# A bidirectional Mamba layer: group 0 of a step on other engines

## The chip, the cores and the metric

The kernel runs on all 8 cores of one Trainium2 chip, each core with one sequence of the batch of 8 and no exchange between them. The metric is the time of the slowest core in microseconds (us), the median of several runs. Lower is better. A core has TensorE (PE, matmuls), VectorE (DVE), ScalarE (ACT), GpSimd (POOL) and the SyncE queue (SP), from which most DMAs are issued here. Each follows its own queue of instructions in order; semaphores tie the queues together.

## The reference

Layer norm, a forward and a backward Mamba block, a projection of both, and a gate from a feed-forward net with ternary weights:

```
xz = x @ win.T;  u, z = split(xz)
u = silu(causal_conv4(u) + bconv)
dbc = u @ wx.T            # dt (64 columns), B (16), C (16)
delta = softplus(dt @ wdt.T + bdt)
dA  = exp(delta[..., None] * A)
dBu = (delta * u)[..., None] * B[:, :, None, :]
h = dA_t * h + dBu_t ;  y_t = sum_n h[:, n] * C_t[n]      # scan over 2048 positions
y = (y + u * Dp) * silu(z);  return y @ wout.T

s = concat(mamba_f(xn), flip(mamba_b(flip(xn)))) @ wproj.T + bproj
g = silu(relu(xn @ Wq1.T + b1) @ Wq2.T + b2)     # Wq: weights rounded to -1, 0, 1
out = x + s * g
```

Sizes of a core: 2048 positions, 1024 model columns, 2048 inner channels, 16 states to a channel, 4096 feed-forward columns.

## The kernel before

Positions are cut into 4 chunks of 512 (`TC`), inner channels into 16 tiles of 128 partitions (`NET`). A **step** s is one channel tile of one chunk of one direction: 2 x 4 x 16 = 128 steps (`NSTEP`), forward first. The 16 states of a step are four **groups** of four (`g` = 0 to 3, `G` = 4 s + g), and a group is two **halves** (pairs) of two states, 1024 columns. Chunks after the first of a direction start from the states carried over from the chunk before ("carried" steps, 96 of 128).

For one group the work is:

- `exp_dA` (L597): ScalarE writes exp(delta A) for each state to one PSUM bank; banks 0 to 3 are two pairs, used in turn by the halves. Column `first(s)` of a state is left at zero, so that a scan over two states starts anew at the second.
- `dbu_half` (L574): GpSimd multiplies `du` (delta times u, from `du_mul`, L562, on VectorE) by B, which lies broadcast over partitions in `Bsl`, into the slot of the group in `hb` (4 slots of 2048 bf16 columns). `fix_b`, `fix_c`, `fix_add` (L622 to L638) add the carried states at the first column.
- `scan` (L648): VectorE, dA from PSUM, dBu and the result in `hb`.
- `h_carry` (L661) saves the last column (ScalarE; VectorE for group 3), `c_mul` (L677) multiplies the slot by C on VectorE, 2048 columns in place, and `y_acc` (L692) sums the four states into PSUM bank `YB` with identity matmuls.
- After group 3, `gate` (L708) multiplies by silu(z) on VectorE.

Around it runs the rest, placed by hand in the main loop (for `s`, for `g`): the u and z projections of later steps (`u_mm`, `z_mm`: 8 matmuls each), the convolution by diagonals (`conv_mm`), delta two steps ahead (`delta_mm`, `delta_exp`: a clamp and an exponential, `delta_ln`), `dbc_mm` and the broadcasts of B and C once a chunk, and in the background the feed-forward net and the output projection (`pe_units`, one unit of 8 matmuls to a group, its result taken out by ScalarE from `act_evacs`) and the rounding of the weights (`act_stream`, ScalarE, 192 operations). Nothing is scheduled by a program at run time: each engine's queue is the order of the calls. `dbu_half` waits for a given C product (its argument `Gc`), which keeps GpSimd's products behind VectorE's.

The order of the main loop around the change, per group G: two exponentials; evacuations, `u_silu`, `z_silu` and others by group; two exponentials; background unit; in group 0 `du_mul(s + 1)`, `h_carry`, `c_mul(G - 1)`, `y_acc(G - 1)` and then `scan(G, 0)`, in the others first `scan(G, 0)` and then `c_mul(G - 1)`; halves on GpSimd; projections; `scan(G, 1)`.

## Time and profile before

| | us |
|---|---|
| timed runs, median of 3 | 3321.85 |
| lowest and highest | 3310.32, 3322.79 |
| profiled execution, its own time | 3301.36 |
| its span on the slowest core (core 4), first to last instruction | 3299.8 |
| spans of the eight cores | 3280.2 to 3299.8 |
| granted TensorE clock, means of the cores | 0.859 to 0.868 |
| busy in the span: DVE, ACT, POOL, PE | 3143.7, 2514.8, 2314.8, 2262.8 |

An engine's busy share is an average over 128 steps and what lies around them. To see what a change in one place is worth, one reads a step in the timeline of the engines: what an instruction waited for, and what its engine did from the end of one to the start of the next. The names of the groups are those of the program: `hb<-ps,hb` is written to `hb` and reads `ps` (PSUM) and `hb`. Instructions are pipelined, so the start of the next lies up to 0.08 us before the end of the one ahead; costs are best read from start to start.

### The profile page before, as it was taken

To read this page: it belongs to the slowest core of one execution; us is meant where nothing else is said; L and a number is where in the kernel's file an instruction comes from. 1 tells how busy PE (TensorE), PEld (TensorE's weight loads), DVE (VectorE), ACT (ScalarE), POOL (GpSimd) and SP (SyncE) were. 2 spreads that over 40 slices of the span, in tenths; PEclk is the share of its full clock that TensorE was granted. 3 is DMA by queue.
4 is the path that set the end of the run, shared out by engine and by line. 5 is a ranking of instruction groups with operands and counts; after the bars stand their busy time and mean duration, and the time that the engine had idled before them with its cause. 6 is when DMAs were issued, how large, how long until landed. Compare 5 with 4: busy or idle time off the path is not lost.

```text
span 3299.8 us, 37727 instructions; the slowest of 8 cores (3280.2 to 3299.8 us)
## 1 busy us (share of the span) xinstructions
PE 2262.8 (69%) x8945; PEld 893.8 (27%) x9124; DVE 3143.7 (95%) x2075; ACT 2514.8 (76%) x4176; POOL 2314.8 (70%) x1545
## 2 busy tenths in 40 slices
PE   6456776777745666667777777677676777777776
PEld 2222222222211222222222223222222223222322
DVE  4899998999999999999999999999999999999997
ACT  4678898998988988877777777777777776666662
POOL 1578776776677776877777777777767777677672
PEclk9678888898987878789889999899898988888987
DMA  9679767554553446533243322322232242534334
GB/s 221 172 143 175 173 144 170 121 164 140 145 163 94 135 122 155 157 86 99 74 126 103 101 86 93 115 78 91 69 109 93 78 134 92 191 130 150 124 123 137
DMA packets 329913, 418.84 MB, mean 127 GB/s; under 512 B 76000, under 2 KB 250720, under 8 KB 318432
## 3 DMA queue, kind: packets, MB, share of 16 engines
q1 hardware_dynamic: 301728, 381.11, 38.5%
q0 software_dynamic: 26960, 34.91, 7.5%
q8 instruction: 79, 1.29, 0.2%
q14 instruction: 138, 1.13, 0.1%
q10 hardware_dynamic: 1008, 0.40, 0.1%
HBM read 374.42 MB, written 76.81 MB: 137 GB/s over the span
## 4 chain that ended last, share of the span: by engine, by line
DVE 36%; ACT 27%; issue 20%; PE 11%; DMA 4%; POOL 1%; DVEq 0%; ACTq 0%; SPq 0%; POOLq 0%
DVE hb L658 24%; ACT ps L613 13%; DVE hb L683 10%; PE ps L373 4%; PE ps L704 2%; ACT L613 2%; ACT L447 2%; PE ps L423 1%; ACT hcar L674 1%; DMA arena<-w2t_sl 1%; ACT arena L768 1%; PE ps L912 1%; ACT ps L548 1%; POOL hb L585 1%; DVE yb L713 1%
## 5 line engine op out<-in xcount | busy, mean ns | idle before, releaser
L585 POOL TENSOR_TENSOR hb<-du,Bsl 128x1024 bf16<-128x1024 bf16 x1024 | 2162.1, 2124 | 798.0 <-DVE hb L683 746.8
L658 DVE TENSOR_TENSOR_SCAN hb<-ps,hb 128x1024 bf16<-128x1024 f32 x1024 | 2299.4, 2273 | 35.5 <-ACT ps L613 34.8
L613 ACT ACTIVATE ps<-delta,A_sb 128x511 f32<-128x511 bf16 x2048 | 1314.9, 678 | 383.6 <-DVE hb L658 380.7
L704 PE MATMUL ps<-hb,ident 128*128 128x512 bf16 x2000 | 629.1, 443 | 902.0 <-DVE hb L683 884.1
L683 DVE TENSOR_TENSOR hb<-hb,Csl 128x2048 bf16<-128x2048 bf16 x512 | 659.3, 1288 | 42.0 <-ACT hcar L674 30.2
L373 PE MATMUL ps<-xn,win 128*128 128x512 bf16 x1871 | 556.3, 447 | 6.5 <-issue 3.7
L704 PEld LDWEIGHTS ps<-hb,ident 128*128 128x128 bf16 x2048 | 184.6, 104 | 1274.3 <-issue 1163.1
L373 PEld LDWEIGHTS ps<-xn,win 128*128 128x128 bf16 x1920 | 208.4, 113 | 323.3 <-issue 193.9
L912 PE MATMUL ps<-xn,slab 128*128 128x512 bf16 x1009 | 254.5, 395 | 17.9 <-ACT big L921 16.6
L935 PE MATMUL ps<-big,slab 128*128 128x512 bf16 x1002 | 252.1, 393 | 1.4 <-issue 0.2
L998 PE MATMUL ps<-big,slab 128*128 128x512 bf16 x751 | 191.6, 409 | 7.5 <-DVE arena L1025 6.2
L674 ACT ACTIVATE hcar<-hb 128x4 f32<-128x4 bf16 x288 | 58.3, 202 | 146.3 <-DVE hb L658 144.5
L613 ACT ACT_TABLE_LOAD x127 | 162.9, 1283 | 3.8 <-DVE du L565 0.4
L447 ACT ACT_TABLE_LOAD x110 | 141.1, 1283 | 11.6 <-PE ps L433 8.4
L888 PE MATMUL ps<-big,slab 128*128 128x512 bf16 x500 | 131.0, 405 | 15.4 <-ACT ev L897 13.9
L912 PEld LDWEIGHTS ps<-xn,slab 128*128 128x128 bf16 x1024 | 98.8, 101 | 155.9 <-issue 58.5
L935 PEld LDWEIGHTS ps<-big,slab 128*128 128x128 bf16 x1024 | 101.5, 101 | 129.4 <-issue 20.3
L423 PE MATMUL ps<-uraw,diagc 128*128 128x512 bf16 (+3 forms) x445 | 123.3, 389 | 0.2
L921 ACT ACTIVATE big<-ps,bcols_s 128x512 bf16<-128x512 f32 x128 | 86.0, 672 | 44.3 <-PE ps L912 44.3
L998 PEld LDWEIGHTS ps<-big,slab 128*128 128x128 bf16 x768 | 79.2, 105 | 113.4 <-issue 38.2
L551 ACT ACTIVATE spe<-ps,cst 128x512 bf16<-128x512 f32 x128 | 87.9, 687 | 11.8
L644 POOL TENSOR_TENSOR hb<-hb,acar 128x4 bf16<-128x4 bf16 (+1 forms) x288 | 65.2, 227 | 41.3
(91 smaller groups left out, 1771.1 us busy)
## 6 DMA issues: line engine op xcount, KB each, us to landing
win<-winq SPq DMA_DIRECT2D x176, 256.0 KB, 2.8
arena<-w1t_sl SPq DMA_DIRECT2D x64, 512.0 KB, 6.4
slab<-w1q SPq DMA_DIRECT2D x32, 1024.0 KB, 5.2
arena<-w2t_sl SPq DMA_DIRECT2D x64, 512.0 KB, 5.4
slab<-w2q SPq DMA_DIRECT2D x32, 1024.0 KB, 5.6
slab<-wp_scr SPq DMA_DIRECT2D x24, 1024.0 KB, 5.4
winq<-win SPq DMA_DIRECT2D x64, 256.0 KB, 2.9
Bsl<-bc_scr SPq DMA_DIRECT2D x32, 512.0 KB, 6.2
```

Source lines behind the costliest of these rows:

```text
L373: e.matmul(out=o, lhsT=w, rhs=r, start=st, stop=sp),
L423: e.matmul(out=o, lhsT=w, rhs=i, start=st, stop=sp),
L447: e.activation(out=o, in_=i, func=AF.Silu, bias=bc), sA)
L585: e.tensor_mul(out=o, in0=a1, in1=Bsl[:, (q % 5) * 2048 + h_ * 1024: (q % 5) * 2048 + (h_ + 1) * 1024] .rearrange("p (n t) -> p n t", n=2) ...
L613: a=A_sb[:, col:col + 1]: e.activation(out=o, in_=d, func=AF.Exp, scale=a), sA)
L658: scan_v[pi] = b.op("vector", lambda e, h=h, a=a: e.tensor_tensor_scan(out=h, data0=a, data1=h, initial=0.0, op0=ALU.mult, op1=ALU.add), sV)
L683: e.tensor_mul(out=o, in0=o, in1=i), sV)
L704: e.matmul(out=bank(YB), lhsT=ident[:], rhs=r, start=False, stop=sp), sPE if n == GN - 1 else None)
L888: e.matmul(out=bank(MB), lhsT=w, rhs=r, start=(k == 0), stop=(k == NKD - 1)), sPE if k == NKD - 1 else None)
L912: r=xn_sl(k, c * TC, TC): e.matmul(out=bank(MB), lhsT=w, rhs=r, start=(k == 0), stop=(k == NKD - 1)),
L935: e.matmul(out=bank(MB), lhsT=w, rhs=r, start=st, stop=sp),
L998: e.matmul(out=bank(bk), lhsT=w, rhs=r, start=st, stop=sp),
```

## The change

For **group 0 of each step**: 

- The increments delta u B are no longer made by GpSimd. `du` is transposed by a DMA (`duT_turn`), and TensorE multiplies it by diagonal matrices of B (`e_mm`: 8 matmuls of 128 columns for a half, and two of one column that add the carried states) into the PSUM banks of the half. The diagonals, 16 blocks of 128 columns for a chunk, are made once a chunk by ScalarE (`diagB_build`), from a transposed B.
- dA goes to the `hb` slot instead, and `scan` takes its two inputs exchanged.
- The C product is made by GpSimd in two halves (`ce_half`).

For all groups: dA is written over all 512 columns, and delta at the first column is set to 1e36 by GpSimd (`delta_far`), so that exp gives zero there. In steps below 56 the clamp before the exponential of softplus (ScalarE) becomes a minimum after it (`delta_min`, VectorE). `du` has two slots instead of three. The main loop is written out by group; the scan of group 0 now comes first in a step, ahead of the C product of group 3 of the step before; the rounding operations are spread, one to a group and two in group 3. The backward projection weights are cast in DRAM by 8 DMAs (`win_cast`) in steps 18 to 39 instead of through SBUF, and the layer norm of chunk 1 moves into the first projections.

```diff
+        def delta_min(s):
+            b.wait("vector", sp_e[s])
+            sp_e[s] = b.op("vector", lambda e: e.tensor_scalar(
+                out=spe[:], in0=spe[:], scalar1=math.exp(SPCAP), scalar2=None, op0=ALU.min), sV)
...
+        def duT_turn(s):
+            b.wait("sync", du_t[s], e_pe.get((s - 1, 1)))
+            duT_t[s] = turn(sDuT, duT[:], du_sl(s), 4)
...
+        def e_mm(s, p_):
+            j, et, fwd, c, half = info(s)
+            pi = 2 * s * NG + p_
+            o = (pi % 2) * 1024
+            cr = carried(s)
+            b.wait("tensor", duT_t[s], t_diagB[j], scan_v.get(pi - 2),
...
+                   fixc_t[s] if cr else None)
+            for k in range(4):
+                for n in range(2):
+                    tok = b.op("tensor", lambda e, k=k, n=n: e.matmul(
+                        out=ps[:, o + n * TC + k * P:o + n * TC + (k + 1) * P],
+                        lhsT=duT[:, k * P:(k + 1) * P],
+                        rhs=diagB_sl(j)[:, (8 * p_ + 2 * k + n) * P:(8 * p_ + 2 * k + n + 1) * P],
...
+        def ce_half(s, h_):
+            G = s * NG
+            q = s // NET * NG
+            b.wait("gpsimd", scan_v[2 * G + h_], hcar_a.get(G), t_C[q])
+            cmul_v[G] = b.op("gpsimd", lambda e, o=hb_sl(G)[:, h_ * 1024:(h_ + 1) * 1024],
+                             i=Csl[:, (q % 5) * 2048 + h_ * 1024:(q % 5) * 2048 + (h_ + 1) * 1024]:
+                             e.tensor_mul(out=o, in0=o, in1=i), sP)
...
+            if g == 0:
+                b.wait("scalar", dl_rdy[s], far_t[s], yacc_pe.get(G - 4))
+                dst = hb_sl(G)[:, n * TC:(n + 1) * TC]
+            else:
+                b.wait("scalar", dl_rdy[s], far_t[s], scan_v[pi - 2])
+                dst = bank(bk)
...
+            d0, d1 = a, h
+            if g == 0:
+                b.wait("vector", e_pe[(s, p_)])
+                d0, d1 = h, a
```

The calls on the queues of VectorE, GpSimd and TensorE in the new main loop, without those of ScalarE:

```
group 0   e_mm(s, 1); scan(G0, 0); h_carry, c_mul, y_acc (G0 - 1); background
          du_mul(s + 1); duT_turn(s + 1); scan(G0, 1); delta_mm, u_mm; gate(s - 1)
          delta_far, fix_c (s + 1); dbu_half(G0 + 2, 1); fix_add(s, 2)
group 1   scan(G0 + 1, 0); ce_half(s, 0); ce_half(s, 1); dbu_half(G0 + 3, 0); fix_add
          background; scan(G0 + 1, 1)
group 2   scan(G0 + 2, 0); background; y_acc(G0); c_mul, y_acc (G0 + 1); delta_min(s + 2)
          z_mm, conv_mm; scan(G0 + 2, 1); dbu_half(G0 + 3, 1); fix_add; dbu_half(G0 + 5, 0)
group 3   scan(G0 + 3, 0); e_mm(s + 1, 0); c_mul, y_acc (G0 + 2); background
          scan(G0 + 3, 1); dbu_half(G0 + 5, 1); fix_add; dbu_half(G0 + 6, 0)
```

**VectorE, one step**, before (scans are L658, here named by their instruction's kind, the C product L683, `du` L565, the carry cast L671, `gate` L713):

```order
L565 TENSOR_TENSOR du<-delta,uring 128x512
L671 CAST hcar<-hb 128x4
L683 TENSOR_TENSOR hb<-hb,Csl 128x2048
L658 SCALAR_TENSOR_TENSOR hb<-ps,hb 128x1024
L713 TENSOR_TENSOR yb<-ps,zb 128x512
L658 SCALAR_TENSOR_TENSOR hb<-ps,hb 128x1024 x2
L683 TENSOR_TENSOR hb<-hb,Csl 128x2048
L658 SCALAR_TENSOR_TENSOR hb<-ps,hb 128x1024 x2
L683 TENSOR_TENSOR hb<-hb,Csl 128x2048
L658 SCALAR_TENSOR_TENSOR hb<-ps,hb 128x1024 x2
L683 TENSOR_TENSOR hb<-hb,Csl 128x2048
L658 SCALAR_TENSOR_TENSOR hb<-ps,hb 128x1024
```

The same engine and a step of the new kernel (scans L812, C product L837, `du` L657, `delta_min` L641):

```order
L812 SCALAR_TENSOR_TENSOR hb<-hb,ps 128x1024
L825 CAST hcar<-hb 128x4
L837 TENSOR_TENSOR hb<-hb,Csl 128x2048
L657 TENSOR_TENSOR du<-delta,uring 128x512
L812 SCALAR_TENSOR_TENSOR hb<-hb,ps 128x1024
L867 TENSOR_TENSOR yb<-ps,zb 128x512
L812 SCALAR_TENSOR_TENSOR hb<-ps,hb 128x1024 x3
L837 TENSOR_TENSOR hb<-hb,Csl 128x2048
L641 TENSOR_SCALAR spe<-spe 128x512
L812 SCALAR_TENSOR_TENSOR hb<-ps,hb 128x1024 x2
L837 TENSOR_TENSOR hb<-hb,Csl 128x2048
L812 SCALAR_TENSOR_TENSOR hb<-ps,hb 128x1024
```

Three C products instead of four; `du` stands behind one, with four scans and the gate product between it and the next.

**GpSimd, one carried step**, before (halves L585, `fix_add` L644, `fix_c` L636):

```order
L585 TENSOR_TENSOR hb<-du,Bsl 128x1024 x2
L644 TENSOR_TENSOR hb<-hb,acar 128x4
L585 TENSOR_TENSOR hb<-du,Bsl 128x1024 x2
L644 TENSOR_TENSOR hb<-hb,acar 128x4
L636 TENSOR_TENSOR acar<-acar,hcar 128x16
L585 TENSOR_TENSOR hb<-du,Bsl 128x1024 x4
L644 TENSOR_TENSOR hb<-hb,acar 128x8
```

And in the new kernel (halves L722, C halves L738, `delta_far` L663, `fix_c` L783, `fix_add` L793):

```order
L663 MEMSET delta 128x1
L783 TENSOR_TENSOR acar<-acx,hcar 128x16
L722 TENSOR_TENSOR hb<-du,Bsl 128x1024
L793 TENSOR_TENSOR hb<-hb,acar 128x4
L738 TENSOR_TENSOR hb<-hb,Csl 128x1024 x2
L722 TENSOR_TENSOR hb<-du,Bsl 128x1024
L793 TENSOR_TENSOR hb<-hb,acar 128x2
L722 TENSOR_TENSOR hb<-du,Bsl 128x1024
L793 TENSOR_TENSOR hb<-hb,acar 128x2
L722 TENSOR_TENSOR hb<-du,Bsl 128x1024 x2
L793 TENSOR_TENSOR hb<-hb,acar 128x4
L722 TENSOR_TENSOR hb<-du,Bsl 128x1024
```

Four halves, two of them C halves, now stand between `du` and the C product of group 1, where two stood behind each C product.

**TensorE, end of a step**, new kernel (z projection L410, convolution L460, `e_mm` L690 and L699, y sums L858); before, the sums of group 2 stood behind one background unit after the convolution:

```order
L410 MATMUL ps<-xn,win 128x512 x8
L460 MATMUL ps<-uraw,diagc 128x512
L460 MATMUL ps<-uraw,diagc 128x511
L460 MATMUL ps<-uraw,diagc 128x510
L460 MATMUL ps<-uraw,diagc 128x509
L690 MATMUL ps<-Bsl,duT 128x128 x8
L699 MATMUL ps<-acar,ident 128x1 x2
L858 MATMUL ps<-hb,ident 128x512 x4
```

The matmuls that open the next step's group 0 stand behind the projection and the convolution, and the sums of group 2 behind them.

## Rows read from the trace of the kernel before

**Rows 1.** Busy times on the page: engine, us, share, instructions
```profile
PE 2262.8 (69%) x8945; PEld 893.8 (27%) x9124; DVE 3143.7 (95%) x2075; ACT 2514.8 (76%) x4176; POOL 2314.8 (70%) x1545
```

**Rows 2.** Groups of the page (busy, mean ns; idle before)
```profile
L585 POOL TENSOR_TENSOR hb<-du,Bsl 128x1024 bf16<-128x1024 bf16 x1024 | 2162.1, 2124 | 798.0 <-DVE hb L683 746.8
L658 DVE TENSOR_TENSOR_SCAN hb<-ps,hb 128x1024 bf16<-128x1024 f32 x1024 | 2299.4, 2273 | 35.5 <-ACT ps L613 34.8
...
L683 DVE TENSOR_TENSOR hb<-hb,Csl 128x2048 bf16<-128x2048 bf16 x512 | 659.3, 1288 | 42.0 <-ACT hcar L674 30.2
```

**Rows 3.** Timeline of VectorE, one step: start us, duration, what
```profile
2178.11 0.42 DVE L565 TENSOR_TENSOR du<-delta,uring 128x512 bf16<-128x512 bf16 x1
2178.46 0.19 DVE L671 CAST hcar<-hb 128x4 f32<-128x4 bf16 x1
2178.75 1.23 DVE L683 TENSOR_TENSOR hb<-hb,Csl 128x2048 bf16<-128x2048 bf16 x1
...
2182.10 0.67 DVE L713 TENSOR_TENSOR yb<-ps,zb 128x512 bf16<-128x512 f32 x1
2182.68 4.46 DVE L658 TENSOR_TENSOR_SCAN hb<-ps,hb 128x1024 bf16<-128x1024 f32 x2
2187.05 1.20 DVE L683 TENSOR_TENSOR hb<-hb,Csl 128x2048 bf16<-128x2048 bf16 x1
2188.17 4.46 DVE L658 TENSOR_TENSOR_SCAN hb<-ps,hb 128x1024 bf16<-128x1024 f32 x2
2192.55 1.63 DVE L683 TENSOR_TENSOR hb<-hb,Csl 128x2048 bf16<-128x2048 bf16 x1
...
2201.81 0.42 DVE L565 TENSOR_TENSOR du<-delta,uring 128x512 bf16<-128x512 bf16 x1
```

**Rows 4.** Timeline of GpSimd in the same step
```profile
2188.40 2.12 POOL L585 TENSOR_TENSOR hb<-du,Bsl 128x1024 bf16<-128x1024 bf16 x1 [1.60 <-DVE hb L683]
2190.66 0.21 POOL L644 TENSOR_TENSOR hb<-hb,acar 128x4 bf16<-128x4 bf16 x1
2190.81 0.22 POOL L636 TENSOR_TENSOR acar<-acar,hcar 128x16 f32<-128x16 f32 x1
2190.99 2.12 POOL L585 TENSOR_TENSOR hb<-du,Bsl 128x1024 bf16<-128x1024 bf16 x1
```

**Rows 5.** Stretch of 400 us: busy us (instructions) by engine, TensorE clock, DMA share, GB/s
```profile
400.00:800.00 400.00, 288.40 (x1126) 110.83 (x1147) 375.87 (x238) 362.88 (x596) 287.27 (x192) 0.89 0.59 147
```

**Rows 6.** Line 585: ns min/median/max, first and last start us
```profile
L585 POOL TENSOR_TENSOR hb<-du,Bsl x1024: 2103/2120/3132, 84.9 to 3247.3; 128x1024 bf16<-128x1024 bf16 x171
```

**Rows 7.** Groups by line, of the smaller operations: busy us, mean ns
```profile
L548 ACT ACTIVATE ps<-ps,cb 128x512 f32<-128x512 f32 x128 | 83.5, 652 | 0.9 <-PE ps L539 0.9
...
L433 PE MATMUL ps<-utail,diagc 128*128 128x1 bf16 (+2 forms) x288 | 47.8, 166 | 0.0
...
L1017 PE MATMUL ps<-ident,arena 128*128 128x128 bf16 x128 | 13.3, 230 | 10.2 <-DVE arena L1009 8.4 <-DVE arena L1112 1.6
```

**Rows 8.** Timeline of TensorE, ends of two convolutions and one z projection
```profile
642.83 0.17 PE L433 MATMUL ps<-utail,diagc 128*128 128x3 bf16 x1
...
666.08 3.10 PE L373 MATMUL ps<-xn,win 128*128 128x512 bf16 x8
...
669.93 0.17 PE L433 MATMUL ps<-utail,diagc 128*128 128x3 bf16 x1
```

**Rows 9.** Two short stretches, columns as in the 400 us stretch above
```profile
666.00:670.00 4.00, 4.00 (x16) 1.58 (x16) 4.00 (x3) 4.00 (x9) 2.95 (x2) 0.68 0.87 303
640.00:643.00 3.00, 3.00 (x18) 1.42 (x17) 3.00 (x2) 3.00 (x7) 3.00 (x2) 1.00 0.46 165
```

**Rows 10.** Timeline of VectorE, last scans of the same two steps
```profile
644.63 2.28 DVE L658 TENSOR_TENSOR_SCAN hb<-ps,hb 128x1024 bf16<-128x1024 f32 x1
...
670.06 2.28 DVE L658 TENSOR_TENSOR_SCAN hb<-ps,hb 128x1024 bf16<-128x1024 f32 x1
```

**Rows 11.** DMA issues: count, KB each, median us to landing
```profile
y_scr<-yb SPq DMA_DIRECT2D x128, 128.0 KB, 2.8
```

More of the change, by code:

```diff
@@ new lines, in build_program @@
+            if s >= 1:
+                gate(s - 1)
+            if et == NET - 1 and j + 1 < 2 * NCH:
+                bc_load_B(j + 1, 1)
+                bc_load_B(j + 1, 2)
+            if 18 <= s < 42 and s % 3 == 0:
+                win_cast((s - 18) // 3)
+            if more:
+                delta_far(s + 1)
+                if carried(s + 1):
+                    fix_c(s + 1)
+            dbu_half(G0 + 2, 1, *opened)
+            if carried(s):
+                fix_add(s, 2, 0, 1)
+            group(1)
@@ new lines, in build_program @@
+            h_carry(G0)
+            exp_dA(G0 + 1, 2)
+            exp_dA(G0 + 1, 3)
+            scan(G0 + 1, 0)
+            ce_half(s, 0)
+            ce_half(s, 1)
+            dbu_half(G0 + 3, 0)
+            if carried(s):
+                fix_add(s, 3, 0)
+            while casts:
+                casts.pop(0)()
+            evacs()
+            quant(1 if s > 4 else 0)
+            if jd is not None and not last_u:
+                dbc_mm(jd, MB)
+            pe_background(1)
+            if s == NSTEP - 1:
+                assert un[0] == "end"
+                y_load(0, 1, 1, 0, NET - 1)
@@ new lines, in build_program @@
+            exp_dA(G0 + 2, 0)
+            exp_dA(G0 + 2, 1)
+            scan(G0 + 1, 1)
+            if newb is not None:
+                bT_copy(newb)
+            if s + 2 < NSTEP:
+                delta_exp(s + 2, s < NQ)
+            evacs()
+            for a in us:
+                u_evac(a)
+            if last_u:
+                dbc_evac(jd, MU)
+            group(2)
+            scan(G0 + 2, 0)
+            h_carry(G0 + 1)
+            exp_dA(G0 + 2, 2)
+            exp_dA(G0 + 2, 3)
@@ new lines, in build_program @@
+            if more:
+                z_mm(s + 1)
+            for a in us[:1]:
+                conv_mm(a)
+            for a in us[1:]:
+                conv_mm(a, MB)
+            scan(G0 + 2, 1)
+            dbu_half(G0 + 3, 1, *opened)
+            if carried(s):
+                fix_add(s, 3, 1)
+            dbu_half(G0 + 5, 0)
+            group(3)
+            scan(G0 + 3, 0)
+            if s + 2 < NSTEP:
+                delta_ln(s + 2)
+                if carried(s + 2):
+                    fix_b(s + 2)
```

514 lines of the change are left out of this document (314 added, 200 removed).

## The prediction

> **What bounds the kernel now.** I read the page's busy times first: VectorE (DVE) is busy 95% of the span, ScalarE 76%, GpSimd (POOL) 70%, TensorE 69% [rows 1]. The costliest groups say what VectorE does: 1024 scans of 2273 ns and 512 C products of 1288 ns, eight and four of each in every one of the 128 steps; GpSimd does 1024 half products delta u B of 2124 ns [rows 2]. Then one step with no wait for ScalarE or TensorE in it: from one `du` product to the next 23.70 us (2178.11 to 2201.81) [rows 3]. Scan to scan it takes 2.19 to 2.20 us (two scans from 2182.68 to the product at 2187.05, 4.37), a C product takes 1.12 us from its start to the next scan (2187.05 to 2188.17). The product at 2192.55 takes 1.63 instead of 1.20 us. GpSimd shows why. The C product ends at 2188.25; GpSimd starts at 2188.40, 0.15 later, gets to the small addition after 2.26, past the two small operations after 0.15 and 0.18 more, and ends the second half product at 2193.11 [rows 4]: 4.86 us in all, against 4.37 for the two scans beside it. The late half holds up the next C product by some 0.44 us. So the scans run undisturbed beside GpSimd, while a C product and a GpSimd product do not run together. Taking that 0.44 out, VectorE alone needs 23.26 us a step; so I count the 32 steps that carry nothing and have no small operations. ScalarE is second: between 400 and 800 us it is busy 363 of 400 us [rows 5], and the scans waited 34.8 us for it in all [rows 2].
>
> **The change, part by part.**
>
> *VectorE loses the C product of group 0.* 128 products, 1.12 us each from start to start, 143 us; at the group's mean of 1288 ns, which holds waits for GpSimd, 165 [rows 2, 3]. It gains a minimum over 512 bf16 columns in 56 steps. No row shows it. The cast of 4 columns takes 0.19 us, the du product of 512 columns 0.42 [rows 3]. I take 0.25, since it reads one operand where du reads two: 14 us (10 to 24). VectorE alone then needs 22.14 us a step, 22.39 with the minimum.
>
> *The scan of group 0 with its operands exchanged.* dA comes from SBUF, the increment from PSUM; still one operand in each. All 1024 scans are of one form, so the trace doesn't show the other. I take 2.27 us, for the same two memories are read and the elements are the same. A gain of more than 0.1 us has no ground, a loss as of a scan with both operands in SBUF (blocked by GpSimd) has none either, since one stays in PSUM.
>
> *GpSimd keeps eight halves.* Two delta u B halves go, two C halves come. Same size and type, so I take 2.12 us; the B halves run from 2.10 to 3.13 [rows 6], which are the bounds. GpSimd also gains a memset of one column and one small addition, 0.15 each [rows 4]. What matters is how they interleave. Its queue in a carried step is now: from the end of `du`, 0.15 to start, memset 0.15, carry product 0.18, half 2.26 and addition 0.15, two C halves 4.20, half 2.26 and the addition's own 0.21, in all 9.56; I round to 9.5. Beside it VectorE runs four scans and the gate product, from du's end to the C product of group 1: 0.35 - 0.42 + 4 x 2.19 + 0.58 = 9.27. GpSimd is 0.2 later. Then the C product and minimum, 1.12 + 0.2 = 1.3, and 0.15 + 2.26 + 0.15 + 2.12 = 4.68 on GpSimd against 4.37 for two scans: together 5.95 against 5.7. Then a C product, and 4.68 again against two scans and the carry cast (0.29 from its start to the C product [rows 3]), 4.66: a tie, 5.79. The longer ones, counted from du's start, with 1.12 for the last C product: 9.92 + 5.95 + 5.79 + 1.12 = 22.8 us, 22.6 without the minimum. Steps that carry nothing stay with VectorE at 22.39 and 22.14.
>
> Against 23.70 and 23.26 before: 16 steps without carried states and with the minimum x 0.87, 40 carried with it x 0.90, 8 carried without x 1.10, 16 with neither x 1.12, 48 carried without x 1.10 = **129 us gained**, not the 143 that leave VectorE: the rest goes to waits for GpSimd.
>
> *TensorE gains 2048 matmuls of 128 columns and 384 of one.* The transposes of the output, of the same size, are busy 13.3 us for 128, so 0.104 us each at mostly full clock; the one-column ones 47.8 us for 288, 0.166 [rows 7]. That is 213 + 64 = 277 us on an engine that is idle a third of the time [rows 1]. By itself it costs nothing. But eight of them now stand on VectorE's path: the scan that opens a step waits for them, and they stand behind the z projection and the convolution, which start when the C product of group 1 ends. Between 666 and 670 us the granted clock is 0.68, partly the lower level (1.2 GHz), the z projection takes 3.10 us, and the last convolution matmul ends at 670.10 [rows 8, 9]; the last scan of the step ends at 672.34 [rows 10]: 2.24 us left. One step earlier, at the higher level (2.4 GHz), it is 643.00 and 646.91, 3.91 left. The eight and two matmuls need 1.2 us at the high clock, up to twice that at the low one. They fit, just. Who pays is GpSimd: the four matmuls that sum group 2 into y now stand behind them, 4 x 0.39 = 1.55 us at the low clock, and the last GpSimd half of the step (group 2 of the next step) waits for that sum, since it writes the same buffer. At the low clock: z and convolution end about when the C product of group 2 ends, then 1.6 + 1.55 = 3.2 us; GpSimd wants to begin after 0.15 + 2.26 + 0.15 = 2.56. So 0.6 to 0.7 us late, handed on to the next C product. At the high clock nothing. I take it in half of the steps, 0.6 x 64 = **38 us lost**; the bounds are none and all steps at 0.9, 0 to 115.
>
> *ScalarE* loses the clamp of 652 ns in 56 steps [rows 7], 37 us, and gains 112 copies of 128 columns, 22 us if each is like VectorE's small ones, 0.2. Its rounding operations are spread one to a group, and the exponentials of group 0 no longer wait for a PSUM bank. Between 400 and 800 us it needs 363/400 of a 25 us step, 22.7; less 0.65 plus 0.17 that is 22.2, close to the 22.8 us of the new step. I cost the two effects at nothing: less work and looser waits against a shorter step. If that cover fails it is 0.5 us in some 40 steps, 20 us.
>
> *DMA.* A transposing DMA of `du` (128 KB) has to land between the du product and the first matmul of the next step. No row shows one. A plain store of 128 KB lands 2.8 us after issue [rows 11]. From du's end to the start of the next step is 22.7 - 4.0 = 18.7 us, less 1.5 for the matmuls: 17 us. I cost it at nothing, from 2.8 us up to 17.
>
> The Trainium skill gives, in "VectorE: DVE Perf Modes", section "The three transpose paths", 1309 ns for a transposing DMA of 128x128; an estimate from that page for four blocks one after another is 5.2 us, which would hide too. No row here shows it.
>
> *Start.* The layer norm of the second chunk leaves the stretch before the first scan, but the transposed copy of du queues behind seven loads of 512 KB. I count nothing, plus or minus 9 us.
>
> **Sum.** Span 3299.8 - 129 + 38 = 3209 us, with the 1.6 us around it (profiled execution 3301.4) 3210. The median of the timed runs before, 3321.85, lies 20.5 above that execution; the same for the new kernel gives **3231 us**, 2.7% less.
>
> **The rivals.**
> - *The GpSimd ring isn't the longer one*: the C halves, or the handoffs, are shorter than I count and TensorE's lateness is absorbed. All of 143 to 165 us is kept, less 14: 3175 us. For it: the order gives GpSimd a place after each C product. Against: the 1.63 us row, which is there already with fewer small operations.
> - *TensorE's backlog decides*: the step's opening matmuls and the sums behind them are late in every step, 0.7 to 0.9 us, 90 to 115 us instead of 38: 3283 to 3308 us, down to no change. For it: 2.24 us of room against up to 2.4. Against: 3.9 us of room in the others.
> - *Slower: the transposing DMA comes late.* It has 17 us; each us beyond costs a us a step, 128 us. The gain of 0.9 a step is gone at 18, and at 20 us the time is 3231 + 3 x 128 = 3615 us. For it: the DMA engines are busy 0.59 of the time between 400 and 800 us [rows 5], and the queue holds megabyte loads. Against: plain transfers of this size take 3 us.
> - *Slower: a C half costs more than a B half.* It reads two full operands where the other repeats one of them. At 0.5 us more, the ring grows by 1.0 to 23.8 and the kernel is slower, 3231 + 128 = 3360 us; from 0.35 us on it is no faster than before. At the slowest B half's 3.13 us it is 3490. The Trainium skill, "GPSIMD Engine Reference", section "4.1 Engine selection", advises VectorE for elementwise work on a tile, GpSimd being about twice as slow with two inputs. The rows here say 4.2 against 1.2 us for 2048 columns, more than that page; it speaks against the move only if GpSimd has no room, and the two halves it gives up make the room.
>
> **Chances.** Forecast (3190 to 3265) 0.56; ring not binding 0.13; backlog 0.16; late DMA 0.07; costlier half 0.08. Range for 8 in 10: 3165 to 3300. About 0.5% (17 us) is what a measurement of this kernel can tell from no change. Faster by more: 0.56 + 0.13 + 0.10 of the backlog case = 0.79; within it the rest of that case and 0.01, 0.07; slower, the last two cases less that 0.01, 0.14.
>
> **What the profile after would show.** VectorE's product count 384, and a carried step of 22.6 to 22.8 us where nothing waits; the C product of group 1 delayed behind GpSimd; C halves on GpSimd at 2.12 us; the opening scan without idle time before it, or with it behind the 128-column matmuls (backlog); GpSimd waiting for the y sums of group 2 in low-clock steps. A mean step above 24 us, or idle time before the matmuls that ends with the transposing DMA, makes the prediction wrong.

## The result, and the profile after

The changed kernel takes **3222.4 us** (median of 4 runs, 3221.72 to 3225.89), the kernel before 3322.3 beside it. The ratio is 0.971, 95% interval 0.969 to 0.973: 2.9% faster. The forecast was 3231 us, range 3165 to 3300. The profiled execution takes 3222.3 us; its span on the slowest core, core 6, is 3220.4, where before it was 3299.8. The spans of the cores lie between 3195.6 and 3220.4. In some executions of each kernel the cores of one die show a lower granted clock and take longer: ratios and medians below leave out those that are over 1% longer for it, and in a trace with one such die the cores of the other are read.

Busy times and the costliest groups of the page, to be laid beside [rows 1, 2]:

```profile
PE 2339.5 (73%) x11337; PEld 1041.7 (32%) x11556; DVE 3012.5 (94%) x2003; ACT 2504.1 (78%) x4237; POOL 2385.0 (74%) x1745
...
L722 POOL TENSOR_TENSOR hb<-du,Bsl 128x1024 bf16<-128x1024 bf16 x768 | 1630.6, 2126 | 330.4 <-DVE hb L837 224.5
L812 DVE TENSOR_TENSOR_SCAN hb<-ps,hb 128x1024 bf16<-128x1024 f32 x768 | 1715.8, 2273 | 45.4 <-ACT hcar L828 33.8
...
L812 DVE TENSOR_TENSOR_SCAN hb<-hb,ps 128x1024 bf16<-128x1024 bf16 x256 | 581.0, 2270 | 38.3 <-PE ps L690 20.7
L738 POOL TENSOR_TENSOR hb<-hb,Csl 128x1024 bf16<-128x1024 bf16 x256 | 538.3, 2124 | 61.1 <-ACT hcar L828 56.3
...
L837 DVE TENSOR_TENSOR hb<-hb,Csl 128x2048 bf16<-128x2048 bf16 x384 | 522.4, 1360 | 29.2 <-ACT hcar L828 18.5
```

The scan with its operands exchanged takes 2270 ns, the other 2273. A C half takes 2124 ns on GpSimd, a B half 2126. GpSimd's idle time behind C products fell from 746.8 to 224.5 us.

One carried step without the minimum, on VectorE (start, duration, what), beside [rows 3]:

```profile
2171.35 0.42 DVE L657 TENSOR_TENSOR du<-delta,uring 128x512 bf16<-128x512 bf16 x1
2171.69 2.28 DVE L812 TENSOR_TENSOR_SCAN hb<-hb,ps 128x1024 bf16<-128x1024 bf16 x1
2173.88 0.67 DVE L867 TENSOR_TENSOR yb<-ps,zb 128x512 bf16<-128x512 f32 x1
2174.46 6.64 DVE L812 TENSOR_TENSOR_SCAN hb<-ps,hb 128x1024 bf16<-128x1024 f32 x3
2181.02 1.20 DVE L837 TENSOR_TENSOR hb<-hb,Csl 128x2048 bf16<-128x2048 bf16 x1
2182.14 4.47 DVE L812 TENSOR_TENSOR_SCAN hb<-ps,hb 128x1024 bf16<-128x1024 f32 x2
2186.52 1.48 DVE L837 TENSOR_TENSOR hb<-hb,Csl 128x2048 bf16<-128x2048 bf16 x1
...
2192.29 0.40 DVE L825 CAST hcar<-hb 128x4 f32<-128x4 bf16 x1
2192.80 1.23 DVE L837 TENSOR_TENSOR hb<-hb,Csl 128x2048 bf16<-128x2048 bf16 x1
2193.94 0.42 DVE L657 TENSOR_TENSOR du<-delta,uring 128x512 bf16<-128x512 bf16 x1
```

From `du` to `du` 22.59 us (before 23.70). The same step on GpSimd, beside [rows 4]:

```profile
2171.89 0.10 POOL L663 MEMSET delta<- 128x1 bf16 x1 [1.81 <-DVE du L657]
2172.01 0.22 POOL L783 TENSOR_TENSOR acar<-acx,hcar 128x16 bf16<-128x16 f32 x1
2172.19 2.12 POOL L722 TENSOR_TENSOR hb<-du,Bsl 128x1024 bf16<-128x1024 bf16 x1
2174.45 0.21 POOL L793 TENSOR_TENSOR hb<-hb,acar 128x4 bf16<-128x4 bf16 x1
2174.60 4.21 POOL L738 TENSOR_TENSOR hb<-hb,Csl 128x1024 bf16<-128x1024 bf16 x2
2178.76 2.13 POOL L722 TENSOR_TENSOR hb<-du,Bsl 128x1024 bf16<-128x1024 bf16 x1
2181.03 1.25 POOL L793 TENSOR_TENSOR hb<-hb,acar 128x2 bf16<-128x2 bf16 x1
...
2188.14 2.12 POOL L722 TENSOR_TENSOR hb<-du,Bsl 128x1024 bf16<-128x1024 bf16 x1 [1.22 <-DVE hb L837]
```

GpSimd's long stretch ends at 2180.89, just before the C product of group 1 at 2181.02. That product is not held; the small addition behind the half is, 1.25 us for 0.20. Held on VectorE are the product of group 2 (1.48 us for 1.20) and the cast (0.40 for 0.14 to 0.20).

**Where the 79 us of the span came from.** The starts of the scans that open the steps, on core 4 before and core 6 after (the slowest of each), give the mean step in each stretch, the last one up to the scan that opens step 127:

| | before | after | us in all |
|---|---|---|---|
| first scan starts at | 99.1 | 117.3 | +18 |
| mean step, steps 0 to 15 | 26.19 | 27.67 | +24 |
| steps 16 to 31 | 25.48 | 25.08 | -6 |
| steps 32 to 127 | 24.35 | 23.13 | -115 |

So the last 96 steps alone gained more than the 129 - 38 = 91 of the sum, and the first 32 with the start gave 36 back. The means over all eight cores say the same: +16, +23, -6 and -116. The start on VectorE, first `du` of step 0:

```profile
98.90 0.42 DVE L657 TENSOR_TENSOR du<-delta,uring 128x512 bf16<-128x512 bf16 x1 [6.26 <-ACT delta L650]
99.24 2.35 DVE L1335 TENSOR_TENSOR Bsl<-ident,bTh 128x1024 bf16<-128x1024 bf16 x2
117.30 2.29 DVE L812 TENSOR_TENSOR_SCAN hb<-hb,ps 128x1024 bf16<-128x1024 bf16 x1 [15.71 <-PE ps L690]
```

And on TensorE, the matmuls that this scan waits for:

```profile
116.18 1.01 PE L690 MATMUL ps<-Bsl,duT 128*128 128x128 bf16 x8 [20.93 <-DMA duT<-du]
```

`du` of step 0 is ready at 99.3, its transposed copy only at 116. And `du` itself is late: the projections now contain the layer norm of chunk 1, which waits for loads of x.

In steps 0 to 15 it is ScalarE. The first operation of the rounding (L897) reads the weights of the feed-forward net, first w1, then w2. Its waits for their loads, in us and times:

```profile
  DMA arena<-w1t_sl: 41.7, 9
  DMA arena<-w2t_sl: 11.9, 7
```

The same operation in the kernel before (L743, core 4):

```profile
  DMA arena<-w2t_sl: 7.8, 3
  DMA arena<-w1t_sl: 1.7, 2
```

All 41.7 us of the waits for w1 lie in the first 560 us, that is in steps 0 to 15.

One such case in ScalarE's timeline:

```profile
222.89 1.06 ACT L897 ACTIVATE arena<-arena 128x1024 bf16<-128x1024 f32 x1 [7.10 <-DMA arena<-w1t_sl]
```

And in VectorE's:

```profile
225.44 2.29 DVE L812 TENSOR_TENSOR_SCAN hb<-hb,ps 128x1024 bf16<-128x1024 bf16 x1 [4.01 <-ACT hb L757]
```

The second rounding operation of group 3 waits 7.10 us for its weights, the exponentials of the next step's group 0 stand behind it, and the scan that opens the step is 4.01 us late.

### The profile page after: what moved, and what is told of

Same layout as the page of the kernel before. It is cut to its first block, busy times and chain, and to the rows that moved or that the text cites. A ratio compares the mean times of both kernels' runs of the same rounds, so it can differ in the third digit from the quotient of the medians.

```text
span 3220.4 us, 43721 instructions; the slowest of 8 cores (3195.6 to 3220.4 us)
## 1 busy us (share of the span) xinstructions
PE 2339.5 (73%) x11337; PEld 1041.7 (32%) x11556; DVE 3012.5 (94%) x2003; ACT 2504.1 (78%) x4237; POOL 2385.0 (74%) x1745
## 4 chain that ended last, share of the span: by engine, by line
DVE 28%; issue 23%; PE 21%; ACT 18%; DMA 6%; POOL 2%; SPq 1%; DVEq 1%; ACTq 0%; another core or an unknown queue 0%; POOLq 0%
DVE hb L812 19%; ACT ps L757 6%; PE ps L410 5%; DVE hb L837 5%; PE ps L858 4%; PE ps L1066 3%; ACT hb L757 2%; PE ps L1152 2%; PE ps L690 1%; DMA arena<-w1t_sl 1%; DVE yb L867 1%; DMA wp_scr<-ev 1%; PE ps L460 1%; SPq L72 1%; POOL hb L722 1%
## 5 line engine op out<-in xcount | busy, mean ns | idle before, releaser
L722 POOL TENSOR_TENSOR hb<-du,Bsl 128x1024 bf16<-128x1024 bf16 x768 | 1630.6, 2126 | 330.4 <-DVE hb L837 224.5
L812 DVE TENSOR_TENSOR_SCAN hb<-ps,hb 128x1024 bf16<-128x1024 f32 x768 | 1715.8, 2273 | 45.4 <-ACT hcar L828 33.8
L757 ACT ACTIVATE ps<-delta,A_sb 128x512 f32<-128x512 bf16 x1536 | 991.3, 683 | 203.3 <-DVE hb L812 198.6
L858 PE MATMUL ps<-hb,ident 128*128 128x512 bf16 x1956 | 572.0, 423 | 559.2 <-DVE hb L837 416.1
L812 DVE TENSOR_TENSOR_SCAN hb<-hb,ps 128x1024 bf16<-128x1024 bf16 x256 | 581.0, 2270 | 38.3 <-PE ps L690 20.7
L738 POOL TENSOR_TENSOR hb<-hb,Csl 128x1024 bf16<-128x1024 bf16 x256 | 538.3, 2124 | 61.1 <-ACT hcar L828 56.3
L837 DVE TENSOR_TENSOR hb<-hb,Csl 128x2048 bf16<-128x2048 bf16 x384 | 522.4, 1360 | 29.2 <-ACT hcar L828 18.5
L410 PE MATMUL ps<-xn,win 128*128 128x512 bf16 x1883 | 513.1, 418 | 4.9 <-issue 1.8
L858 PEld LDWEIGHTS ps<-hb,ident 128*128 128x128 bf16 x2048 | 188.0, 102 | 801.2 <-issue 664.7
L757 ACT ACTIVATE hb<-delta,A_sb 128x512 bf16<-128x512 bf16 x512 | 331.8, 712 | 0.8 <-POOL delta L663 0.8
L1066 PE MATMUL ps<-xn,slab 128*128 128x512 bf16 x1000 | 276.5, 423 | 52.7 <-ACT big L1075 51.2
L410 PEld LDWEIGHTS ps<-xn,win 128*128 128x128 bf16 x1920 | 194.0, 106 | 280.0 <-issue 114.0
L663 POOL MEMSET delta<- 128x1 bf16 x128 | 13.0, 102 | 320.8 <-DVE du L657 319.5
L690 PE MATMUL ps<-Bsl,duT 128*128 128x128 bf16 x2048 | 157.7, 220 | 110.7 <-DVE hb L812 77.4
L690 PEld LDWEIGHTS ps<-Bsl,duT 128*128 128x128 bf16 x2048 | 127.1, 98 | 177.8 <-issue 149.4
L793 POOL TENSOR_TENSOR hb<-hb,acar 128x2 bf16<-128x2 bf16 (+1 forms) x384 | 140.9, 367 | 55.6 <-POOL hb L722 0.9
L1066 PEld LDWEIGHTS ps<-xn,slab 128*128 128x128 bf16 x1024 | 106.5, 106 | 204.2 <-issue 112.7
```

Of the source, the lines that this page charges most:

```text
L410: e.matmul(out=o, lhsT=w, rhs=r, start=st, stop=sp),
L690: tok = b.op("tensor", lambda e, k=k, n=n: e.matmul(out=ps[:, o + n * TC + k * P:o + n * TC + (k + 1) * P], lhsT=duT[:, k * P:(k + 1) * P] ...
L722: e.tensor_mul(out=o, in0=a1, in1=Bsl[:, (q % 5) * 2048 + h_ * 1024: (q % 5) * 2048 + (h_ + 1) * 1024] .rearrange("p (n t) -> p n t", n=2) ...
L738: e.tensor_mul(out=o, in0=o, in1=i), sP)
L757: e.activation(out=o, in_=d, func=AF.Exp, scale=a), sA)
L793: e.tensor_add(out=o, in0=o, in1=a), sP)
```

## The experiments

Ratios are to runs of the kernel before on the same chip; the changed kernel's is 0.971. The chips differ between the groups of runs, so ratios compare better than times do.

### One cause of the early loss at a time

The doubled rounding operation back to group 1:

```diff
-            quant(1 if s > 4 else 0)                  # group 1
+            quant((2 if s > 4 else 1) if s else 0)
...
-            quant(1 if s else 0)                      # group 3, the second one
```

> The second rounding operation of group 3 goes back to group 1, so that a step has them at 2, 1, 1 as the kernel before had; nothing else changes. Theory A (in the first steps ScalarE stands behind a rounding operation whose 512 KB load is issued too late, 41.7 us of waits for the w1 loads, and VectorE then waits for exponentials): those waits fall under 10 us, the first 16 steps lose some 30 us, 3192 us. Theory B (the first steps are slow because the queue of DMAs is held by the store of projection weights, whatever the order of the rounding): under 5 us of change, 3222 us. It also tests whether the spreading that the change made was worth anything in steps 16 to 50: if it was, these steps grow by 0.3 us or more.

Measured: ratio 0.974 (0.970 to 0.979), median 3226 us: no gain over the changed kernel's 0.971. In the profiled execution die 0 had a granted clock of 0.845 to 0.860; the spans of die 1 (0.888 to 0.890) are 3195.5 to 3205.0, median 3203, against 3211 for the changed kernel's die 1. The trace shows both halves of the story. On core 6 the first 16 steps fell from 29.2 and 26.1 (8 each) to 26.6 and 25.0, 30 us. But steps 16 to 47 rose from 25.0, 25.2, 23.1, 23.1 to 25.5, 26.5, 23.9, 23.5, and gave 23 us back. The rounding's wait for w1 fell from 41.7 to 4.9 us, and that for w2 rose from 11.9 to 27.4. The queue that issues the loads had waited for this rounding operation in turn: 31.0 us in 8 cases between 115 and 345 us, and 3.6 in 2 here. Theory B had the size of the total, but not its cause: the later steps did lose it again, at another load.

The layer norm of chunk 1 behind the projections, as in the kernel before:

```diff
-            if a == 10:
-                ln_stats(1)
-            if a >= 12:
-                ln_norm(a - 8)
...
-        e_mm(0, 0)
...
+        ln_chunk(1)
         for i in range(10, 16):
             ln_load(i)
+        e_mm(0, 0)
```

> The layer norm of chunk 1 goes back behind the first projections, and the first opening matmuls stand behind its transposes on TensorE; the rest as in the changed kernel. Theory A (the norm moved forward waits for x, which has not landed, and ScalarE and TensorE stand behind it: 18 us): first scan at 99 us instead of 117, 3204 us. Theory B (the transposed copy of du behind seven broadcast loads sets the first scan): first scan stays above 112 us, 3220 us.

Measured: ratio 0.967 (0.964 to 0.971), median 3204 us, as theory A said. The first scan begins at 98 to 109 us by core, instead of 113 to 119. (In this profiled execution both dies had a low granted clock, 0.775 to 0.794; the run below shows the same start without that.)

Both edits (`e1_rounding` and `e2_norm` together):

> Both edits of the two runs before it. If their losses are separate they add up: 3222 - 30 - 18 = 3174 us. If both are one shortage of DMA time in the first 400 us, the second brings less than half of what it brings alone: 3190 us.

Measured: ratio 0.964 (0.962 to 0.967), median 3194 us, spans 3178.7 to 3192.0: 28 less than the changed kernel's on the slowest core. VectorE's first scan on core 6:

```profile
98.87 2.29 DVE L812 TENSOR_TENSOR_SCAN hb<-hb,ps 128x1024 bf16<-128x1024 bf16 x1 [3.24 <-PE ps L690]
```

The waits of the rounding on core 4 (us, times):

```profile
  DMA arena<-w2t_sl: 21.6, 7
  DMA arena<-w1t_sl: 5.4, 5
```

By stretches, core 4 of this kernel against core 6 of the changed one (the slowest of each): the first scan starts at 104.5 instead of 117.3, 13 less; steps 0 to 15 take 26.05 and 24.60 (8 each), together 37 less; steps 16 to 47 take 25.8, 26.5, 23.7, 23.5, 25 more. -13 - 37 + 25 = -25; the span shows 28 less, and the other 3 lie in the later steps. So the sum of the two full gains (3174) wasn't reached for the same reason as in the first run. The number of the other theory, 3190, is nearer, but its cause isn't what the trace shows: the second edit kept its gain, and the loss lies behind step 16.

With the clamp on ScalarE in every step (`NQ = 0` instead of 56) on top:

> As the run with both edits, and softplus clamped on ScalarE in all steps, as before the change (no minimum on VectorE). Theory A (ScalarE is nearly full in steps 8 to 31): 56 x 0.65 us more on it costs more than the 56 x 0.2 us that VectorE saves, 10 us slower than the run with both edits, 3184 us. Theory B (VectorE alone sets these steps): 11 us faster, 3163 us.

Measured: ratio 0.967 (0.963 to 0.970), median 3198 us, 4 us above the kernel of both edits, and the two intervals overlap. Theory B's 11 us less would be a ratio of 0.961, which lies outside: it is out. The 10 us of theory A show in the two profiled executions (the median of the eight spans is 12 us above), but not in the others, where those medians differ by 2 to 5 us. The stretches, means over the eight cores of the profiled executions: the first 32 steps are 14 us longer in all, steps 32 to 47 2 us shorter, and the rest is the same. On core 4 alone it is 8 us longer and, in steps 32 to 55, 5 us shorter. So the direction is theory A's: up to step 31 ScalarE sets the step and the minimum on VectorE is worth its price, and from step 32 on it costs a little. Its size isn't settled beyond 4 to 12 us.

### What the C product is worth, and who has room

The C product of group 0 back on VectorE:

```diff
-            ce_half(s, 0)
-            ce_half(s, 1)
-            dbu_half(G0 + 3, 0)
+            c_mul(G0)
+            dbu_half(G0 + 3, 0, cmul_v[G0])
```

> The changed kernel with the C product of group 0 back on VectorE, as one product over 2048 columns behind the first scan of group 1; the increments by TensorE, dA in SBUF and all else stay. Theory A (the gain is the 1.12 us a step that leave VectorE, less what GpSimd holds up): VectorE alone then needs 23.26 us in a carried step without the minimum, 23.46 with it, where the changed kernel takes 22.59; with 0.2 to 0.4 us of held products it is 23.3 to 23.8, 0.7 to 1.1 more in each of 128 steps, 3222 + 90 to 140 = 3310 to 3360 us, no faster than the kernel before. GpSimd, with two halves less, waits over 4 us more a step. Theory B (the gain comes from the new order and the looser waits of ScalarE, not from the product): it stays within 30 us of the changed kernel, 3222 to 3250.

Measured: 3312 us, ratio **1.001** (0.998 to 1.004): no faster than before. The products of groups 0, 1 and 2 in VectorE's timeline of this kernel:

```profile
2173.16 1.20 DVE L837 TENSOR_TENSOR hb<-hb,Csl 128x2048 bf16<-128x2048 bf16 x1
2174.28 4.46 DVE L812 TENSOR_TENSOR_SCAN hb<-ps,hb 128x1024 bf16<-128x1024 f32 x2
2178.66 1.20 DVE L837 TENSOR_TENSOR hb<-hb,Csl 128x2048 bf16<-128x2048 bf16 x1
...
2184.16 1.46 DVE L837 TENSOR_TENSOR hb<-hb,Csl 128x2048 bf16<-128x2048 bf16 x1
```

And the largest wait of GpSimd's B halves (224.5 us in the changed kernel):

```profile
  DVE hb L837: 829.2, 316
```

The step is 23.71 us (`du` at 2167.85 and 2191.56), 1.12 more than 22.59: just the product. The stretches tell the rest (core 6 of both kernels). In steps 32 to 127 the changed kernel's mean step is 0.91 us shorter, 86 us; in steps 0 to 31 it is 29.2, 26.1, 25.0, 25.2 against 28.6, 26.4, 25.0, 24.8, nothing. There VectorE has one product less and gains nothing by it, since ScalarE sets the step.

This kernel also tells what the rest of the change is worth without the product. In steps 32 to 127 its mean step is 24.04 us, where the kernel before has 24.35: 30 us less in all. In these steps VectorE waited 22.7 us for ScalarE's exponentials before (21 times), and 0.6 us here (once). So of the 115 us of the table, 86 are the product's and some 30 come from the other edits, most of them as such waits. The start and steps 0 to 15 take them away again (first scan at 117.6 us, mean step 27.51), and so the whole is no faster than before.

The second C half left out (two of the four states of group 0 go into y without C):

```diff
             ce_half(s, 0)
-            ce_half(s, 1)
...
-            b.wait("tensor", cmul_v[G])
+            b.wait("tensor", cmul_v[G], scan_v[2 * G + 1] if g == 0 else None)
```

> The changed kernel without the second C half of GpSimd in each step: two of the four states of group 0 go into y without being multiplied by C. All else, with y waiting for the scan instead, is the same. Theory A (GpSimd's queue, as a ring with VectorE, sets the step): GpSimd has 2.12 us less of 19, the held operations go, and the step falls from 22.59 to what VectorE needs alone, 22.14 to 22.3, so 28 to 45 us less, 3177 to 3194 us. Theory B (VectorE's own work sets the step, GpSimd has room): no change, 3222 within 10 us. In both the steps below 48, where ScalarE is late, gain nothing.

Measured: 3229.3 to 3262.9 us in five executions, but none with the changed kernel's granted clock (0.879 to 0.891) on both dies; the profiled one, 3229.3, had 0.849 to 0.863. The other four had it on one die (0.885 to 0.894), and there the slowest core took 3196.5 to 3200.3 us, where the changed kernel's slowest core of a die takes 3214 to 3224: some 20 us less. The profiled execution tells where at least 11 of them are. Its first 8 steps take 27.4 us as a mean over the cores, instead of 28.8, and the rounding's waits for w1 are 19.3 us on core 6 instead of 41.7. Neither theory had this, for both left the early steps out, and why the w1 loads come in better time with less work on GpSimd isn't shown. From step 32 on nothing is gained: 23.18 and 23.05 us in steps 32 to 47 against 23.36 and 23.08, and the step itself shows why. VectorE's timeline from the product of group 1 to that of group 2:

```profile
2188.16 1.20 DVE L837 TENSOR_TENSOR hb<-hb,Csl 128x2048 bf16<-128x2048 bf16 x1
2189.28 4.46 DVE L812 TENSOR_TENSOR_SCAN hb<-ps,hb 128x1024 bf16<-128x1024 f32 x2
2193.66 1.46 DVE L837 TENSOR_TENSOR hb<-hb,Csl 128x2048 bf16<-128x2048 bf16 x1
```

GpSimd's beside it:

```profile
2189.51 2.12 POOL L722 TENSOR_TENSOR hb<-du,Bsl 128x1024 bf16<-128x1024 bf16 x1 [3.22 <-DVE hb L837]
2191.78 0.20 POOL L793 TENSOR_TENSOR hb<-hb,acar 128x2 bf16<-128x2 bf16 x1
2191.92 2.12 POOL L722 TENSOR_TENSOR hb<-du,Bsl 128x1024 bf16<-128x1024 bf16 x1
```

The step ahead of these lines is 22.57 us (`du` at 2155.92 and 2178.49), this one 22.59, not shorter by a tenth, though GpSimd has 2.12 us less to do and now waits 3.22 us before its half. The product of group 2 is held as before (1.46 us, 1.48 with both halves). The two B halves beside the scans start only behind the product of group 1, which ends at 2189.36, and need 0.15 + 2.27 + 0.14 + 2.12 = 4.68 us; the scans are done after 4.30. What GpSimd does elsewhere changes nothing in that. So theory A falls for the steps that VectorE sets: what GpSimd costs VectorE there is this one pair and the cast, not its sum of work. Theory A's total, 3177 to 3194, and theory B's, within 10 us of 3222, both miss the some 3200 us of the dies with the same clock.

### TensorE's room

Each of the 8 matmuls of `e_mm` done twice:

```diff
-            for k in range(4):
+            for r, k in [(0, k) for k in range(4)] + [(1, k) for k in range(4)]:
...
```

> The changed kernel with each of the 8 matmuls that make the increments of half a group 0 done twice, into the same banks: 2048 more matmuls of 128 columns, 158 us of TensorE at 0.077 us. Theory A (the matmuls that open a step have room on TensorE, and only the sums of y behind them come late at the lower clock): 0.6 to 1.2 us more before those sums makes GpSimd wait in more steps than the 22 times (28.8 us) now, and the time grows by 10 to 45 us, 3232 to 3267. Theory B (the opening matmuls are the last thing the first scan waits for in most steps): 0.6 us or more in every step, 80 to 130 us, 3300 to 3350, with the scans of group 0 idle behind the 128-column matmuls.

Measured: 3224.0 us, ratio 0.975 (0.971 to 0.979). Against the changed kernel's 0.971 that is 4 us less to 29 more, which the two intervals don't tell from nothing. TensorE's matmuls of this line on core 2, their count doubled (busy, mean ns; idle before):

```profile
L690 PE MATMUL ps<-Bsl,duT 128*128 128x128 bf16 x4096 | 273.4, 220 | 100.8 <-DVE hb L812 71.0 <-DMA duT<-du 20.6 <-ACT zb L495 4.3
```

Theory B, 80 to 130 us, is out. Of theory A the small end is possible, but hardly by its mechanism: on cores 0 and 2 GpSimd waits 22.1 and 23.8 us for y sums, in the changed kernel 23.0 and 21.5. One thing more differs: on die 0 the granted clock is 0.895 to 0.902, where the changed kernel has 0.883 to 0.889, and so the time is that of more matmuls at a slightly higher clock.

The sums of group 2 ahead of the matmuls that open the next step:

```diff
-            if more:
-                e_mm(s + 1, 0)
             c_mul(G0 + 2)
             y_acc(G0 + 2)
+            if more:
+                e_mm(s + 1, 0)
```

> The changed kernel with the sums of group 2 into y ahead of the matmuls that open the next step, instead of behind them. The sums wait for the C product of group 2, which ends 4.4 us before the step does. Theory A (room is short): the opening matmuls start 0.8 to 1.6 us after that product and are done 1.4 to 2.8 us after it, and the scan that opens the step begins 4.4 us after: so they still fit, GpSimd no longer waits for the sums (28.8 us now), and the time falls by 5 to 25 us, 3197 to 3217, or not at all if those waits lie beside others. Theory B (what I took in the prediction's rival, TensorE's backlog decides): projection and convolution end so late that sums and matmuls together pass the end of the step, 0.5 to 1 us late in each, 60 to 120 us slower, 3280 to 3340.

Measured: 3227.3 us, ratio 0.976 (0.972 to 0.980). Theory B is out; there is no gain, and a small loss, up to 31 us, is possible. How long GpSimd's B halves wait for y sums, in the changed kernel (core 6, us, times):

```profile
  PE ps L858: 28.8, 22
```

The same with the sums first:

```profile
  PE ps L858: 27.8, 22
```

And an opening scan with the sums first:

```profile
2189.28 2.29 DVE L812 TENSOR_TENSOR_SCAN hb<-hb,ps 128x1024 bf16<-128x1024 bf16 x1 [0.29 <-PE ps L699]
```

So the matmuls that I had put in front of the sums do not make these waits. Behind the sums the opening matmuls themselves come late: on core 6 the opening scans wait 37.5 us for them in 23 cases, where they wait 22.3 in 4 in the changed kernel. These 15 us fit the small loss.

What does make the waits can be read from the trace of the changed kernel, by which half product waits. Of the 22 on core 6, 4 are of the kind that I forecast, the half of group 2 of the next step behind the sum of group 2 (6.4 us). The other 18 (22.4 us) are another half, that of group 1 of the next step, which waits for the sum of group 1. Steps 88 to 91 have one each. In step 88, first GpSimd and VectorE, then TensorE:

```profile
2254.03 2.12 POOL L722 TENSOR_TENSOR hb<-du,Bsl 128x1024 bf16<-128x1024 bf16 x1 [1.03 <-PE ps L858]
2254.70 2.53 DVE L837 TENSOR_TENSOR hb<-hb,Csl 128x2048 bf16<-128x2048 bf16 x1
```

```profile
2248.37 3.54 PE L1066 MATMUL ps<-xn,slab 128*128 128x512 bf16 x8 [2.01 <-ACT big L1075]
2251.70 0.45 PE L850 MATMUL ps<-uring,diagd 128*128 128x512 bf16 x1
2251.99 1.89 PE L858 MATMUL ps<-hb,ident 128*128 128x512 bf16 x8
```

The sums of groups 0 and 1 (eight matmuls, L858) stand behind a background unit of the feed-forward net (L1066), which had waited 2.01 us for ScalarE and took 3.54 us at a granted clock of 0.72 (2249 to 2254 us). The half starts 1.03 us late, and so the C product of group 2 takes 2.53 us instead of 1.48. These four steps take 23.68 to 23.69 us each, steps 83 to 86 22.58 to 22.59. An estimate from that: 18 such steps at 1.1 us are 20 us, which neither run could give back, since both changed what stands before the other sum.

### A version that is faster than both

Both edits, with the doubled rounding operation in group 1 up to step 15 and in group 3 from 16 on:

```diff
-            quant(1 if s > 4 else 0)                  # group 1
+            quant((2 if s > 4 else 1) if 0 < s < 16 else 1 if s else 0)
...
-            quant(1 if s else 0)                      # group 3, the second one
+            quant(0 if s < 16 else 1)
```

> The changed kernel with the layer norm of chunk 1 behind the projections, and the doubled rounding operation in group 1 up to step 15 (two, one, one over groups 1, 2, 3, as in the kernel of both edits) and in group 3 from step 16 on (one, one, two, as in the changed kernel). Theory A (each place is late where its weight loads are: in steps 0 to 15 the later place waits for loads of w1, 42 us; from step 16 on the earlier one waits for loads of w2, 22 us against 12): the first 16 steps keep what both edits gained (26.1 and 24.6 us a step), and steps 16 to 47 go back from 25.8, 26.5, 23.7 and 23.5 to 25.0, 25.2, 23.1 and 23.1, which is 8 x 3.1 = 25 us: 3194 - 25 = 3169 us, 3160 to 3180. Theory B (ScalarE's work is what it is, and what is gained early is handed back later whatever the place): steps 16 to 47 stay as in the kernel of both edits, 3190 to 3200 us.

Measured: ratio 0.961 (0.957 to 0.965), median 3186, above the 3160 to 3180 of theory A; spans of the profiled execution 3157.6 to 3178.3, their median 3169 against 3189 with both edits alone. The intervals of the two ratios overlap, so the totals don't tell the two kernels apart; the trace is plainer. Steps 16 to 47 on core 4 are 25.6, 25.0, 23.2, 23.1, 21 us less than with both edits, of the 25 expected, and steps 0 to 15 kept theirs (26.1, 24.4). The rounding's waits, core 6 (with both edits alone there 21.5 and 3.1):

```profile
  DMA arena<-w2t_sl: 13.5, 7
  DMA arena<-w1t_sl: 6.8, 4
```

With the minimum in steps 0 to 31 alone (`NQ = 32`):

> The same, with the minimum on VectorE in steps 0 to 31 alone instead of 0 to 55; in the others ScalarE clamps before the exponential. Theory A (from step 32 on VectorE, not ScalarE, sets the step, so the minimum costs there and the clamp doesn't): 24 steps x 0.2 us less, 5 us under the kernel beside it, 3164. Theory B (ScalarE is still short of time in steps 32 to 55): as in the kernel with the clamp everywhere, which was 11 us above the one with the minimum; a share of it, 3 to 6 us slower, 3173 to 3176.

Measured: ratio **0.959** (0.955 to 0.962), median 3179 us; the changed kernel's interval, 0.969 to 0.973, lies above it. Steps 32 to 55 on core 7 are 22.9, 22.9, 22.6 against 23.1, 23.1, 22.7, 4 us less, near the 5 of theory A. Against the kernel beside it the totals don't separate.

## Why the prediction was right, and where it wasn't

The total was 8.6 us off, and that is luck: the errors behind it are several times as large and cancelled. What holds is the step that VectorE sets.

- **VectorE's step: right.** Forecast 22.6 us for a carried step without the minimum, measured 22.59; 1.11 less than before. The run with the product back on VectorE gives 23.71 and the time of the kernel before, so without the product there is no gain.
- **The parts of that step: wrong in two places.** I let GpSimd set the first stretch at 9.92 us from du's start, by counting the addition behind its last half. VectorE needs 9.67 and sets it; the addition is what is held. And I counted 0.3 for the halves beside group 1 and nothing for a held cast; measured are 0.27 before the product of group 2 is through and 0.21 at the cast. The run without the second C half shows that neither comes from that half. The rival of a ring that doesn't bind was right for the first stretch only, and its price wasn't to be had, because the two holds are left (the price, 3175 us, isn't the middle of its own sum either, which gives 3171 to 3193).
- **The minimum.** Taken at 0.25 us, 14 us in all; start to next scan it takes 0.20, 0.287 as the group's mean, 11 us in all. But in steps 0 to 31 the time of ScalarE that it saves was worth more than it cost, by the profiled executions.
- **The term of 38 us for late y sums: wrong in its place.** I had the half of group 2 wait in half the steps, behind the opening matmuls and the sum of group 2. That wait exists 4 times, 6.4 us; with the sums put first 2 of them are left (4.7 us) and no time is gained. The step that failed was to put both behind the projection and the convolution in every step at the low clock: the room of 2.24 us [rows 8, 10] is the short case, and the matmuls take 0.077 us each (157.7 / 2048), not 0.104. In the step shown above (`du` at 2171.35) the convolution ends at 2186.04 and the opening matmuls may start at 2186.75 only. Late sums there are all the same, at group 1 behind a background unit, 18 times, worth some 20 us by the estimate above; I hadn't looked there. The backlog rival falls with it: the opening scans waited 20.7 us for these matmuls in 3 cases, 15.7 of them at the start.
- **ScalarE at nothing: wrong both ways.** In steps 32 to 127 the looser waits that I put at nothing gave most of some 30 us (above). In the early ones this is the step that failed. I had named the price if that cover went (0.5 us in 40 steps, 20 us), and counted the gain of the product in all 128 steps. For steps 0 to 31 I counted 28 us of gain and about 9 of loss; they lost 18. By the run with the product on VectorE, the product is worth nothing there. The sign of it is in [rows 5], which I read as an average over 400 us: 363 of 400 busy is close to full for a queue that also waits. What I did not ask was what is queued behind each rounding operation if its load is late. With two in group 3 it is the exponentials that open the next step.
- **The start: 0 ± 9 forecast, 18 measured** (15.5 as the mean over the cores). I saw that the transposed copy of `du` queues behind loads, but not that a layer norm put among the projections makes them wait for x, nor that the matmuls of delta for step 1 stand behind the opening matmuls of step 0. With the norm moved back (the run of both edits) the first scan is at 98.7 to 104.5 us, mean 101.5, where the kernel before has 100.0.
- **Costlier C half, late transposing DMA: didn't happen.** 2124 ns against 2126. Issued on SP's queue, the transposing DMA takes 1.2 us there and lands 3.4 us after issue (median), 15.4 at the longest. The Trainium skill's 1309 ns for a block (its page "VectorE: DVE Perf Modes", section "The three transpose paths") gave an estimate of 5.2 us for four; the trace has less, so either a block takes less here or they overlap. The Trainium skill, "GPSIMD Engine Reference", section "4.1 Engine selection", has GpSimd about twice as slow as VectorE with two inputs; 4.21 against 1.20 us for 2048 columns is 3.5 times, and the move paid nevertheless, since GpSimd had given up work of the same size.
- **The offset.** I put the median 20.5 us above the profiled execution; here they are the same (3222.4 and 3222.3). That hid an error of 11 us in the span: 3220.4 where I had 3209. Start +18, steps 0 to 31 +36, steps 32 to 127 -43 (115 gained, where the forecast had 101 for VectorE less 28 for the y sums): +11. The 115 are 86 by the product and some 30 by the other edits, mostly waits for ScalarE that went.

## What to carry to other kernels

Multiply a gain on the bounding engine only by the steps in which it bounds; here steps 0 to 31 weren't among them, and ScalarE had been busy 363 of 400 us there. When operations of one queue are spread anew, ask for each that may wait for a load what stands behind it, in each phase of the loads: the best place changed at step 16. And in a ring of two engines look for the pair of handoffs that holds the other side, not for the sum of work: taking 2.1 us from GpSimd took nothing off the steps that VectorE sets. When an instruction waits for a late result, look up which one of its kind waits: the 22 waits for y sums were mostly not the ones that I had forecast.
